# Second layer's softplus: one ScalarE function between two table loads in place of a chain on three engines, and two stages' loops written out

## The reference, cut to what matters

```python
dt = jax.nn.softplus(jnp.einsum('blr,dr->bld', dt_r, dt_w) + dt_b)
A = -jnp.exp(A_log)
def step(h, inp):
    dt_t, x_t, B_t, C_t = inp
    da = jnp.exp(dt_t[..., None] * A)
    h = da * h + (dt_t * x_t)[..., None] * B_t[:, None, :]
    y = jnp.einsum('bdn,bn->bd', h, C_t)
    return (h, y)
```

## Time and profile before

| | |
|---|---|
| median of 3 runs (lowest, highest) | 1646.45 us (1641.7, 1650.43) |
| profiled execution, its span | 1644.6 us (the page gives no other time of it) |
| VectorE busy | 1293.9 us (79%) |
| TensorE busy | 1289.1 us (78%) |
| ScalarE busy | 1163.7 us (71%) |
| GpSimd busy | 971.4 us (59%) |
| `mid1_phase`, about | 721.7 to 1504 us |

### The profile page before, as it was taken

One profiled execution on the slowest core, in us unless ns is written; L12 is line 12 of the kernel. 1 busy time (PEld: TensorE's weight loads), 2 busy tenths in 40 slices (PEclk: granted clock), 3 DMA queues, 4 the chain that ended last, 5 costly groups with the idle time before them and its releaser, 6 DMA issues. The chain is left out here.

```text
span 1644.6 us, 15347 instructions
## 1 busy us (share of the span) xinstructions
PE 1289.1 (78%) x3822; PEld 436.0 (27%) x3822; DVE 1293.9 (79%) x1306; ACT 1163.7 (71%) x1787; POOL 971.4 (59%) x515
## 2 busy tenths in 40 slices
PE   4999766685862777767888898888898888775995
PEld 2344201110100455532222222222222222111563
DVE  1655569999995577711999999999999999994675
ACT  2676368687772577748888988888889888740564
POOL 2400038969697323315898888898888898860000
PEclk8999855555555899978788988888878988655998
DMA  5344460200003133317777777777777776734573
GB/s 155 101 139 130 107 171 0 96 6 13 38 1 109 44 96 96 88 51 169 171 165 160 182 178 175 173 170 173 174 176 174 168 168 145 163 79 101 122 174 75
DMA packets 136423, 200.44 MB, mean 122 GB/s; under 512 B 26739, under 2 KB 68770, under 8 KB 135564
## 3 DMA queue, kind: packets, MB, share of 16 engines
q1 hardware_dynamic: 133740, 196.15, 49.2%
q10 hardware_dynamic: 2160, 2.61, 0.6%
q0 software_dynamic: 448, 0.85, 0.2%
HBM read 145.93 MB, written 53.63 MB: 121 GB/s over the span
## 5 line engine op out<-in xcount | busy, mean ns | idle before, releaser
L1796 DVE TENSOR_TENSOR_SCAN m_h<-m_qa,m_state,m_ub 128x512 f32<-128x512 f32 x384 | 463.9, 1261 | 16.0 <-POOL m_ub L1417 11.6
L1417 POOL TENSOR_TENSOR m_ub<-m_dlb,m_bt 128x1536 f32<-128x1536 f32 x128 | 438.5, 3445 | 16.4 <-DVE m_h L1796 11.4
L1757 ACT ACTIVATE m_qa<-m_dlb,k_a 128x512 f32<-128x512 f32 x384 | 254.2, 682 | 89.3 <-DVE m_h L1796 88.0
L1137 POOL TENSOR_TENSOR b_u<-b_dl,b_z 128x1024 f32<-128x1024 f32 x48 | 125.3, 2610 | 210.9 <-DVE b_dl L1054 210.4
L1610 PE MATMUL m_qc<-m_bcr,k_selc 32*128 32x512 f32 x256 | 167.2, 737 | 99.2 <-DVE m_g L1807 99.0
L1807 DVE TENSOR_TENSOR m_g<-m_h,m_qc 128x1536 f32<-128x1536 f32 x128 | 221.6, 1731 | 11.9 <-issue 6.6
L1627 PE MATMUL m_qy<-m_g,k_seld 128*32 128x512 f32 x768 | 175.1, 767 | 0.0
L984 PE MATMUL b_qb<-b_bc,k_pack_sel 96*128 96x512 bf16 x96 | 81.6, 850 | 73.2 <-DVE b_u L1060 71.0
L1551 PE MATMUL m_qf<-m_cva,k_conv 113*96 113x504 f32 (+1 forms) x192 | 105.0, 689 | 5.0 <-PEq L1171 5.0
L1610 PEld LDWEIGHTS m_qc<-m_bcr,k_selc 32*128 32x128 f32 x256 | 42.7, 208 | 223.2 <-issue 187.2
L1023 ACT ACTIVATE b_qa<-b_dl,b_a 128x1024 f32<-128x1024 f32 x48 | 53.7, 1118 | 61.8 <-DVE b_dl L1054 61.8
(11 more groups left out here) (187 smaller groups left out, 2645.3 us busy)
## 6 DMA issues: line engine op xcount, KB each, us to landing
m_dlb<-scratch_dldu SPq DMA_DIRECT2D x128, 384.0 KB, 10.3
m_bt<-scratch_brow SPq DMA_DIRECT2D x128, 256.0 KB, 5.9
scratch_dldu<-m_dldu SPq DMA_DIRECT2D x32, 384.0 KB, 3.2
scratch_z<-a_z SPq DMA_DIRECT2D x24, 256.0 KB, 6.0
b_z<-scratch_z SPq DMA_DIRECT2D x3, 2048.0 KB, 11.1
scratch_y<-b_yrow SPq DMA_DIRECT2D x12, 512.0 KB, 2.6
c_y<-scratch_y SPq DMA_DIRECT2D x16, 384.0 KB, 3.3
scratch_gate<-m_gt SPq DMA_DIRECT2D x32, 192.0 KB, 3.6
```

What stands on the lines that cost most here:

```text
L1137: nc.gpsimd.tensor_tensor(by_column(u[s][:], col), by_column(dl[s][:], col), seen(z[j % 2][:], col, piece), ALU.mult).then_inc(u_ready, 1)
L1417: nc.gpsimd.tensor_tensor(ub[k % 3][:], dlb[u % 2][:, J:2 * J, :], bcast(bt[u % 2][:, n, :], J), ALU.mult).then_inc(ub_ready, 1)
L1757: nc.scalar.activation(q_a[:, j, :], dlb[u % 2][:, j, :], ACT.Exp, scale=G["a1"][:, j, n:n + 1]).then_inc(da, 1)
L1796: nc.vector.tensor_tensor_scan(h[k % 3][:, j, :], q_a[:, j, :], ub[k % 3][:, j, :], state[:, k % NS, j:j + 1], ALU.mult, ALU.add).then_inc ...
```

## The change

In `mid1_phase` the softplus chain goes. ScalarE loads the table set `softplus`, applies one Softplus activation that reads the PSUM tile and writes `dldu` itself, and loads the Exp set again, all in quarter 3, where `log` stood. `small`, `log` and `rounding` and VectorE's `softplus` are gone, and with them five scratch tiles and two semaphores; `delta`, which counts finished units of dt, is now counted up by ScalarE. Nothing else in `mid1_phase` moves.

In `back0_phase` and `back1_phase` the hardware loop of `in_flight` becomes straight code in the same order; the counts and addresses become constants. Three helpers that nothing called are removed.

```diff
-LOG_EXP_SET, LOG_SET, SILU_SET = "natural_log_exp_and_others", "natural_log", "silu_and_others"
+LOG_EXP_SET, SILU_SET, SOFTPLUS_SET = "natural_log_exp_and_others", "silu_and_others", "softplus"
...
-    def steps(i0, first, exists):
-        for c in first:
-            for ahead, stage in stages:
-                if exists(c + ahead):
-                    stage(eng, i0 + c + ahead, (c + ahead) % slots)
-
-    steps(0, range(-slots, 0), lambda i: i >= 0)
-    with eng.Fori(0, chunks // slots - 1) as turn:
-        steps(slots * turn, range(slots), lambda i: True)
-    steps(chunks - slots, range(slots), lambda i: i < slots)
+    for c in range(-slots, chunks):
+        for ahead, stage in stages:
+            i = c + ahead
+            if 0 <= i < chunks:
+                stage(eng, i, i % slots)
...
-            def rounding(v):
...
-                pool.wait_ge(soft, SOFT * v + SOFT)
-                nc.gpsimd.tensor_tensor(wm[:], wm[:], ep[:], ALU.subtract).then_inc(corr, 1)
-                pool.wait_ge(corr, 2 * v + 1)
-                nc.gpsimd.tensor_tensor(lw[:], lw[:], wm[:], ALU.subtract).then_inc(corr, 1)
...
-            def small(v):
+            def softplus(v):
...
-                    act.wait_ge(corr, 2 * v)
-                    act.wait_ge(delta, v)
+                act.preload_act_table_set(SOFTPLUS_SET)
                 act.wait_ge(dt_mm, v + 1)
-                nc.scalar.activation(ab[:], q_g[0:DI, :], ACT.Abs).then_inc(soft, 1)
-                act.wait_ge(soft, n + 1)
-                nc.scalar.activation(ab[:], ab[:], ACT.Exp, scale=-1.0).then_inc(soft, 1)
-
-            def log(v):
...
-                nc.scalar.activation(w[:], ab[:], ACT.Identity, bias=one).then_inc(soft, 1)
-                nc.scalar.activation(ep[:], ab[:], ACT.Identity, bias=less).then_inc(soft, 1)
-                act.wait_ge(soft, n + 3)
-                nc.scalar.activation(wm[:], w[:], ACT.Identity, bias=minus_one).then_inc(soft, 1)
-                nc.scalar.activation(lw[:], w[:], ACT.Ln).then_inc(soft, 1)
+                if v >= 2:
+                    act.wait_ge(dldu_stored[v % 2], 16 * (v // 2))
+                nc.scalar.activation(dldu[v % 2][:, 0, :], q_g[0:DI, :], ACT.Softplus).then_inc(delta, 1)
+                act.preload_act_table_set(LOG_EXP_SET)
...
                 if s == 2:
                     u_of(t + 4)
-                    small(t + 3)
                 if s == 3:
-                    log(t + 3)
+                    softplus(t + 3)
...
-            def softplus(v):
...
-                dve.wait_ge(corr, 2 * v + 2)
...
-                nc.vector.scalar_tensor_tensor(dldu[v % 2][:, 0, :], q_g[0:DI, :], 0.0, lw[:], ALU.max, ALU.add).then_inc(delta, 1)
```

More of the change, by code:

```diff
@@ L489, in stages_of @@
     return [(place[name][0], stage) for name, stage in sorted(stages.items(), key=lambda item: place[item[0]][1])]
[L492 to L498, removed]
 def dma_done(i, s, n, slots=2):
     return (i - s) * (n // slots) + n
[L506 to L529, removed]
 class Conv:
@@ L1337 @@
 HIST = 5
-SOFT = 6
 def unit(u):
@@ L1357, in mid1_phase @@
         bcr = [m.sb(f"m_bcr{r}", [P, CH]) for r in range(4)]
-        ab, w, ep, wm, lw = (m.sb(f"m_{n}", [DI, CH]) for n in ("ab", "w", "ep", "wm", "lw"))
         dldu = [m.sb(f"m_dldu{r}", [DI, 2, CH]) for r in range(2)]
@@ L1369, in mid1_phase @@
         (zeroed, conv_mm, gate_mm, z_mm, u_mm, dt_mm, skip_mm, c_mm, added,
-         xa_ready, gt_ready, sz_ready, xm_ready, tail, u_out, taps_out, bc_out, soft, da, kept,
-         summed, corr, du_ready, ub_ready, delta, scanned, read, y_ready) = (
+         xa_ready, gt_ready, sz_ready, xm_ready, tail, u_out, taps_out, bc_out, da, kept,
+         summed, du_ready, ub_ready, delta, scanned, read, y_ready) = (
             m.sem(f"m_{n}") for n in (
                 "zeroed", "conv_mm", "gate_mm", "z_mm", "u_mm", "dt_mm", "skip_mm", "c_mm", "added",
-                "xa_ready", "gt_ready", "sz_ready", "xm_ready", "tail", "u_out", "taps_out", "bc_out", "soft", "da", "kept",
-                "summed", "corr", "du_ready", "ub_ready", "delta", "scanned", "read", "y_ready"))
+                "xa_ready", "gt_ready", "sz_ready", "xm_ready", "tail", "u_out", "taps_out", "bc_out", "da", "kept",
+                "summed", "du_ready", "ub_ready", "delta", "scanned", "read", "y_ready"))
         cv_loaded, gt_stored, dldu_stored, dlb_loaded, bt_loaded, y_stored = (
@@ L1429, in conv_sum @@
                 nc.gpsimd.tensor_tensor(acc[:], acc[:], tp[2][:], ALU.add).then_inc(summed, 1)
-            def rounding(v):
-                if not exists(v):
-                    return
-                pool.wait_ge(soft, SOFT * v + SOFT)
-                nc.gpsimd.tensor_tensor(wm[:], wm[:], ep[:], ALU.subtract).then_inc(corr, 1)
-                pool.wait_ge(corr, 2 * v + 1)
-                nc.gpsimd.tensor_tensor(lw[:], lw[:], wm[:], ALU.subtract).then_inc(corr, 1)
             def du_of(v):
@@ L1446, in step @@
             def step(t, s, k):
-                if s == 0:
-                    rounding(t + 2)
                 if s == 2:
@@ L1816, in outputs @@
                 nc.vector.tensor_tensor(yo[v % 2][:], q_y[:], sz[v % 5][:], ALU.mult).then_inc(y_ready, 1)
-            def softplus(v):
-                if not exists(v):
-                    return
-                dve.wait_ge(corr, 2 * v + 2)
-                if v >= 2:
-                    dve.wait_ge(dldu_stored[v % 2], 16 * (v // 2))
-                nc.vector.scalar_tensor_tensor(dldu[v % 2][:, 0, :], q_g[0:DI, :], 0.0, lw[:], ALU.max, ALU.add).then_inc(delta, 1)
             def step(t, s, k):
@@ L1831, in step @@
                 times_c(k - 1)
-                if s == 0:
-                    softplus(t + 2)
             turns(step)
```

7 lines of the change are left out of this document (removed).

## The result

| | before | after |
|---|---|---|
| median of the runs | 1645.9 us (4 runs, 1641.7 to 1650.4) | 1627.9 us (4 runs, 1625.5 to 1634.8) |
| ratio, 95% interval | 1 | 0.9889 [0.9856, 0.9923] |
| profiled execution, span | 1644.6 us | 1623.8 us |

The kernel is 18.0 us (1.1%) faster by the medians, 20.8 by the two profiled spans. Forecast were 1617 and 29.7 us off; 1627.9 lies in the range.

The account below looks back on a forecast made before the run. VectorE was taken to bound the second layer's scans, a chain around the engines the first back stage. Scan stage 25.7 + first back 3.0 + second back 1.0 = 29.7 us off, giving 1617 us, range 1604 to 1634.

Parts of the forecast that it names:

- VectorE's instruction, 18.0 us: Second layer's scans: the softplus instruction removed from VectorE saves 0.60 us in each of 30 units, 18.0 us.
- Waits for exponentials, 4.4 us: Second layer's scans: VectorE's 15 pieces of waiting for ScalarE's exponentials, 4.4 us together, all go.
- The start, 2.3 + 1.0 us: Second layer's start: VectorE's 2.33 us wait for GpSimd's second subtraction goes; the shorter chain before the first scan saves 1.0.
- ScalarE's 3.17 us: Quarter 3 of a scan unit: two table loads and one Softplus take 3.17 us, leaving exponentials 1.7 us of room.
- rival A: Scans: each new table load holds up ScalarE some 1.3 us beyond its row; 27 us lost, about 1644 us; chance 6%.
- rival B: Scans: low TensorE clock falls on products before quarter 3's C rows in every unit; 27 us slower, 1673 us; chance 6%.
- the waits in front of C double: Forecast's worst bound: VectorE's waits before the product with C add 9.6 us, backs and start give nothing; 1631 us.
- back0, 3.0 us: First back stage: written-out loops bring loads sooner, so VectorE's multiplication no longer runs beside GpSimd's addition; 3.0 us saved.
- if the loads come about half a microsecond sooner, the two no longer meet: First back stage: loads about half a microsecond sooner part GpSimd's addition from VectorE's multiplication; at most 4.5 us, 3.0 taken.
- back1, 1.0 us: Second back stage: TensorE waits less for a load queued behind a store; 1.0 us saved, between 0 and 3.

Follow-up runs that it names:

- the loops alone: The kernel before with only the stages' loops written out, old softplus chain kept: 1646.1 us, ratio 1.0010 to the kernel before.

## Why the prediction was right, and where its sizes were off

- **VectorE's instruction, 18.0 us: right.** It is gone from the row, nothing took its place, and put back it costs 0.60 us in each unit (the time rose by more, for TensorE's waits).
- **Waits for exponentials, 4.4 us: 2.9.** They went with the chain, and not with GpSimd's work; one of 1.5 us is left.
- **The start, 2.3 + 1.0 us.** The wait of 2.33 us between the first scans went; two quarters of scans now follow each other. The stretch ahead of the first scan is 2.3 us shorter, which can't be credited to the softplus: the loops alone have it too. So nothing is shown for the 1.0.
- **ScalarE's 3.17 us: 3.20,** with 2.0 us of room against the 1.7 forecast. The table loads cost their rows, which takes rival A away.
- **The term left out: TensorE's waits, +6.8 us.** The prediction named this as rival B and gave it all or nothing (waits in every unit, 66 us), and its range held "the waits in front of C double". What came was a mild form that belonged in the sum. Rival B's condition came about for the most part, long convolution products in 25 of 32 units for 11; its price of 2.2 us did not, as VectorE waited that long behind them once and else 1.4 us or less. Its reason, the shorter period, isn't shown: 13.7 and 30.1 us came with the same VectorE row and the long period.
- **back0, 3.0 us: nothing.** The step that failed is "if the loads come about half a microsecond sooner, the two no longer meet". In the chunk shown the addition did begin 0.50 us sooner, measured from the multiplication, and the two still met, as the addition itself grew from 0.89 to 1.39 us and the one behind it began just ahead of the multiplication as before. The reading beneath it was wrong too: the short multiplication does lie beside an addition, one that began after it (567.12 against 567.10). What counts is which begins first. With GpSimd held back by one wait all 16 were short and the 4 us came.
- **back1, 1.0 us: not shown.** 2.3 in the profile, 0.4 with the loops alone, no difference in the medians.

The forecast was 29.7 us. Less the misses (4.0 for the backs, 1.0 for the start, 1.5 for the exponentials, 6.8 for TensorE) it is 16.4. The scans' stretch shows 17.7 and the medians 18.0. The runs of one kernel scatter over some 10 us, so this is no closer than a few us. That the time came out in the range is therefore owed to the first term and to a range wide enough for the backs to give nothing.

What stays open: what sets the places of the long low stretches, and with it why the new chain brings TensorE's waits of 21 to 30 us where the old one had 14 to 17. In the stretch shown above the DMA share is 1.01 against 0.68 ahead of it; whether transfers have a part wasn't tried.

## What to carry to other kernels

An instruction taken off the engine that sets the pace is worth its row, and that is the term to trust; but ask which engine comes second, at which of its clock levels, and put its growing waits into the sum rather than only among the rivals. When the start of an instruction is compared between two profiles, measure it from its neighbour in the same chunk and not from the start of the program, since all of a stage can lie half a microsecond earlier. Where two engines disturb each other, look at both rows, since either can be the one that grows; moving one behind the other by one wait may be worth more than making it early.

## What the runs showed of the hardware

- TensorE's granted clock was lower where it was given less to do: 0.87 granted with all taps, 0.80 with two left out, 0.93 with two products added (of zero weights); at the end of the stage 0.53 without and 0.92 with products for nobody. Less TensorE work made two kernels 14.6 and 28 us slower.
- Table loads followed activations, and in one experiment each other, within 0.03 us at 1.28 us each, some 130 times; four in one quarter cost four times the row.
- A GpSimd addition of 128x256 and VectorE's 128x768 multiplication, both between SBUF tiles, disturb each other, and the one that begins second pays: the multiplication took 1.45 us for 0.96 when the addition had begun 0.09 us ahead of it (the addition then 0.72), and the addition 1.38 for 0.72 when it began 0.16 us behind (the multiplication then 0.96). In the scans 2.56 us more of GpSimd's work per unit cost 0.1 to 0.2 us by the times.
